# A graph network's gathers and picks: ten picked tiles, fifteen gathered ones with two pauses, and fourteen tiles in split sums

## The reference

```
h = max(layernorm(x), 0)
for i in 0, 1, 2:
    W   = (edge_attr @ ew[i] + eb[i]).reshape(E, 16, 16)
    msg = einsum('ei,eio->eo', h[src], W)
    agg = segment_sum(msg, dst, 12500)
    h   = agg + h @ rw[i] + rb[i]
    i < 2: h = relu(batchnorm(h) * gamma[i] + beta[i])    else: h = relu(h)
out = x + h @ pred_w + pred_b
```

## Time and profile before

| | |
|---|---|
| time, median of 3 runs (lowest to highest) | 7962.36 us (7962.15 to 7968.61) |
| the profiled execution: its own time, its span | 7981.32 us, 7979.3 us |
| granted clock of TensorE, mean of the span | 0.97 |
| TensorE busy | 7599.8 us (95%), 44926 matmuls |
| VectorE busy | 6861.3 us (86%) |
| GpSimd busy | 5874.3 us (74%) |
| ScalarE busy | 5047.8 us (63%) |
| bytes moved by DMA | 219.23 MB, 27 GB/s |

### The profile page before, as it was taken

One profiled execution on the slowest core, in us unless ns is written; L12 is line 12 of the kernel. 1 busy time (PEld: TensorE's weight loads), 2 busy tenths in 40 slices (PEclk: granted clock), 3 DMA queues, 4 the chain that ended last, 5 costly groups with the idle time before them and its releaser, 6 DMA issues.

```text
span 7979.3 us, 122061 instructions
## 1 busy us (share of the span) xinstructions
PE 7599.8 (95%) x44926; PEld 7163.3 (90%) x44926; DVE 6861.3 (86%) x7407; ACT 5047.8 (63%) x8079; POOL 5874.3 (74%) x6010
## 2 busy tenths in 40 slices
PE   6999999999999899999999999989999999999998
PEld 4999999899999699998999999969999999899997
DVE  6999998888888799988888888879998888888885
ACT  5666666666666566666666666656666666666664
POOL 5777777777777577777777777757777777777774
PEclk8999999999999799999999999979999999999998
DMA  4111111111111111111111111111111111111110
GB/s 42 28 28 29 28 29 27 28 28 26 28 28 26 23 30 28 28 28 28 26 28 28 27 27 28 26 24 27 30 28 28 28 28 26 28 28 26 28 26 20
DMA packets 497075, 219.23 MB, mean 27 GB/s; under 512 B 303728, under 2 KB 447728, under 8 KB 496478
## 3 DMA queue, kind: packets, MB, share of 16 engines
q1 hardware_dynamic: 255300, 159.40, 7.9%
q0 software_dynamic: 192000, 49.54, 7.6%
q10 hardware_dynamic: 49178, 2.46, 0.7%
HBM read 207.43 MB, written 3.49 MB: 26 GB/s over the span
## 4 chain that ended last, share of the span: by engine, by line
POOL 61%; issue 19%; PE 18%; DVE 1%; ACT 1%; ACTq 0%; POOLq 0%; DMA 0%; DVEq 0%
POOL xg L439 61%; PE bank L1035 10%; PE bank L991 4%; PE bank L978 1%; PE bank L988 1%; PE bank L1093 1%; PE bank L1105 1%; ACTq L804 0%; PE bank L1007 0%; PE bank L1008 0%; ACT agg L819 0%; POOLq L304 0%; ACTq L805 0%; DVE xp L586 0%; PE bank L1001 0%
## 5 line engine op out<-in xcount | busy, mean ns | idle before, releaser
L439 POOL DMA_INDIRECT xg<-node_table,idx x6000 | 5873.4, 979 | 2025.2 <-issue 1875.4
L1035 PE MATMUL bank<-nodes,low_hot 128*128 128x400 f32 x27000 | 5162.1, 349 | 78.2 <-DVE spread L631 59.2
L1035 PEld LDWEIGHTS bank<-nodes,low_hot 128*128 128x128 f32 x27000 | 4933.5, 190 | 226.9 <-DVE spread L631 129.1
L879 ACT ACTIVATE distance<-key,low_id 128x640 bf16<-128x640 int16 (+1 forms) x3000 | 2076.1, 763 | 108.9 <-ACT low_hot L883 72.9
L883 ACT ACTIVATE low_hot<-distance,one 128x640 fp32r<-128x640 bf16 (+1 forms) x3000 | 2072.1, 763 | 0.0
L631 DVE TENSOR_TENSOR spread<-mask,bank 128x400 f32<-128x400 uint8 x3375 | 1720.7, 566 | 209.8 <-PE bank L1035 209.5
L991 PE MATMUL bank<-xp,hot 128*112 128x144 f32 x13500 | 1719.1, 286 | 0.0
L586 DVE TENSOR_TENSOR xp<-xg,bank 128x3200 f32<-128x3200 f32 x375 | 1306.9, 3485 | 469.8 <-DMA xg<-node_table,idx 467.9
L991 PEld LDWEIGHTS bank<-xp,hot 128*112 128x112 f32 x13500 | 1682.0, 177 | 0.0
L843 ACT ACTIVATE xparts<-cut_room 128x1008 fp32r<-128x1008 f32 x375 | 393.6, 1050 | 1848.1 <-DVE cut_room L655 1848.1
L636 DVE TENSOR_REDUCE xg<-spread 128x80 f32<-128x2000 f32 x750 | 1521.0, 2028 | 25.6
(11 more groups left out here) (104 smaller groups left out, 1573.6 us busy)
## 6 DMA issues: line engine op xcount, KB each, us to landing
key<-edge_keys SPq DMA_DIRECT2D x375, 288.0 KB
xg<-node_table,idx POOLq DMA_INDIRECT x6000
ea<-in_edge_attr SPq DMA_DIRECT2D x375, 64.0 KB
ea<-in_edge_attr SPq DMA_DIRECT2D x375, 36.0 KB
idx<-in_src SPq DMA_DIRECT2D x375, 8.0 KB
node_table<-rows SPq DMA_DIRECT2D x3, 781.2 KB
xp<-node_table SPq DMA_DIRECT2D x9, 192.0 KB
xp<-in_x SPq DMA_DIRECT2D x2, 781.2 KB
```

What stands on the lines that cost most here:

```text
L439: pool.indirect_dma_start(out=xg[u][:, j, :], out_offset=None, in_=table[:, :], in_offset=bass.IndirectOffsetOnAxis(ap=idx[u][:, j:j + 1], ...
L879: nc.scalar.activation(distance[f][:, 0:tiles.stop - tiles.start, :], key[u % KEYS][:, tiles, :], ACT.Abs, bias=low_id[:, f:f + 1]).then_i ...
L1035: last = nc.tensor.matmul(p_sel[t % BANKS], low_hot[:, f, t, :], nodes[i][:, f, :, :].rearrange("p d f -> p (d f)"), start=(f, i) == (0, 1 ...
```

## The change

- One tile more is picked (`PICKED` 10, halves of five and five) and one fewer gathered (15).
- In each slot GpSimd stops ahead of gathers 5 and 12 (`RESTS`) until all gathers issued so far in the slot have landed. From the sixth slot of a layer on (`LEAD` = 5) it then multiplies three tiles with their features, 128x384 each time (`multiply_early`), after waiting for the sums of the slot two earlier; the first six tiles of the slot are made in this way. In the first five slots VectorE multiplies them. SyncE waits for these products too before it loads the next edges into their buffer.
- `CUT` is 14: tiles 6 to 19 are split. Their products have one buffer (`xs`), and are made and cut before the last five tiles are multiplied.
- The rest (lower part) is taken in four rounds of 504 columns. For each round ScalarE copies the upper part to PSUM (`p_cut`), and VectorE subtracts it from the products; a round waits for the one before. The rounds lie between the first four picks of the next slot.
- The transposes come after pick 4 and use bank 0, the messages after pick 7; buffers share room in other ways.

```diff
-PICKED = 9
+PICKED = 10
-CUT = 7
+CUT = 14
+ROUNDS = 4
-PARTS = (slice(0, 5), slice(5, 9))
+PARTS = (slice(0, 5), slice(5, 10))
+RESTS = (5, 12)
+EARLY = 6
+LEAD = SLOTS
...
+        xbig = sb("xbig", [P, CUTS + PAIR * WHOLES])
...
+        p_cut = bank[1][:, 0:ROUND]
...
+            def multiply_early(layer, b, u, i):
+                k = layer * G + b * SLOTS + u
+                here = slice(i * EACH, (i + 1) * EACH)
+                pool.wait_ge(s_seg, k + CREDIT - 1)
+                nc.gpsimd.tensor_tensor(
+                    xw[k % PAIR][:, here, D:D + FD].rearrange("p j (f d) -> p j f d", d=D),
+                    xg[u][:, here, :].unsqueeze(2).to_broadcast([P, EACH, F, D]),
+                    ea[u][:, here, :].unsqueeze(3).to_broadcast([P, EACH, F, D]), ALU.mult).then_inc(s_early, 1)
...
                         for j in range(FETCHED):
+                            if j in RESTS:
+                                pool.wait_ge(s_gath[u], (layer * BODIES + b) * (16 * FETCHED) + 16 * j)
+                                if b * SLOTS + u >= LEAD:
+                                    multiply_early(layer, b, u, RESTS.index(j))
                             pool.indirect_dma_start(
...
-            def multiply(layer, b, u):
+            def multiply_split(layer, b, u):
...
+                dve.wait_ge(s_xg, k * 2 + 1)
+                if k:
+                    dve.wait_ge(s_lower, ROUNDS * k)
+                products(xs, xg[u][:, SPLIT, :], p_ea[k % PAIR][:, SPLIT, :]).then_inc(s_first_prod, 1)
+
+            def multiply_whole(layer, b, u):
...
+                if b * SLOTS + u < LEAD:
+                    products(xw[k % PAIR][:, 0:EARLY, :], xg[u][:, 0:EARLY, :], p_ea[k % PAIR][:, 0:EARLY, :])
+                products(xw[k % PAIR][:, EARLY:, :], xg[u][:, LATE, :], p_ea[k % PAIR][:, LATE, :]).then_inc(s_prod, 1)
+
+            def cut_upper(k):
+                dve.wait_ge(s_xc, 2 * k + 1)
+                dve.wait_ge(s_first_prod, k + 1)
+                if k:
+                    dve.wait_ge(s_upper, k)
+                nc.vector.tensor_scalar(xcut.bitcast(I32), xbig[:, 0:CUTS].bitcast(I32), -(1 << 12), None,
                                         ALU.bitwise_and).then_inc(s_cut, 1)
+            def take_lower(k, r):
+                here = slice(r * ROUND, (r + 1) * ROUND)
+                lower = xparts[:, 1, :, :].rearrange("p a b -> p (a b)")
+                dve.wait_ge(s_round, ROUNDS * k + r + 1)
                 dve.wait_ge(s_seg, k + CREDIT)
+                nc.vector.tensor_tensor(lower[:, here], xbig[:, here], p_cut, ALU.subtract).then_inc(s_lower, 1)
...
             def copy_upper(k):
                 act.wait_ge(s_cut, k + 1)
-                nc.scalar.activation(xparts[:, :, 0, :], xcut, ACT.Copy).then_inc(s_upper, 1)
+                nc.scalar.activation(xparts[:, 0, :, :].rearrange("p a b -> p (a b)"), xcut, ACT.Copy)
+                for r in range(ROUNDS):
+                    if k + r:
+                        act.wait_ge(s_lower, ROUNDS * k + r)
+                    last = nc.scalar.activation(p_cut, xcut[:, r * ROUND:(r + 1) * ROUND], ACT.Copy)
+                    last.then_inc(s_round, 1)
+                act.wait_ge(s_round, ROUNDS * k + ROUNDS)
+                act.sem_inc(s_upper, 1)
...
+                split = range(SPLIT.start, SPLIT.stop)
+                whole = (*range(EARLY), *range(LATE.start, TILES))
+                for j in (*split[:-1], *whole, split[-1]):
```

More of the change, by code:

```diff
@@ L29 @@
 TURNS = 3
+RESTS = (5, 12)
+EARLY = 6
+LEAD = SLOTS
 WIN = 112
 NODE_P = 125
-ROOM = 3
+ROOM = 4
 SUB = 4
@@ L86, in gnn_kernel @@
         ea = [sb(f"ea{u}", [P, TILES, F]) for u in range(SLOTS)]
-        xp = [sb(f"xp{i}", [P, TILES, D + FD]) for i in range(PAIR)]
+        WIDTH = D + FD
+        CUTS, WHOLES = CUT * WIDTH, (TILES - CUT) * WIDTH
+        ROUND = CUTS // ROUNDS
+        SPLIT = slice(EARLY, EARLY + CUT)
+        LATE = slice(EARLY + CUT, TILES)
+        EACH = EARLY // len(RESTS)
+        assert EARLY == EACH * len(RESTS) and all(EACH * (i + 1) <= r for i, r in enumerate(RESTS))
+        assert FETCHED <= SPLIT.stop <= FETCHED + PARTS[0].stop
+        assert CUTS % ROUNDS == 0 and ROUND <= 512
+        xbig = sb("xbig", [P, CUTS + PAIR * WHOLES])
+        xs = xbig[:, 0:CUTS].rearrange("p (a b) -> p a b", b=WIDTH)
+        xw = [xbig[:, CUTS + i * WHOLES:CUTS + (i + 1) * WHOLES].rearrange("p (a b) -> p a b", b=WIDTH)
+              for i in range(PAIR)]
+        x_far = xbig[:, 0:CUTS + WHOLES].rearrange("p (a b) -> p a b", b=WIDTH)
         hot = [sb(f"hot{i}", [P, TILES, WIN], F32R) for i in range(PAIR)]
-        cut_room = sb("cut_room", [P, ROOM, SUB * NODE_P])
-        xcut = cut_room[:].rearrange("p a b -> p (a b)")[:, 0:CUT * (D + FD)].rearrange("p (a b) -> p a b", b=D + FD)
-        xparts = sb("xparts", [P, CUT, 2, D + FD], F32R)
+        cut_room = sb("cut_room", [P, CUTS])
+        xcut = cut_room[:]
+        assert ROOM * SUB * NODE_P <= CUTS
+        xparts = sb("xparts", [P, 2, CUT, WIDTH], F32R)
         xg = [sb(f"xg{u}", [P, TILES, D]) for u in range(SLOTS)]
-        key = [sb(f"key{i}", [P, PICKED, P], I16) for i in range(KEYS)]
+        key_all = sb("key_all", [P, KEYS, PICKED, P], I16)
+        key = [key_all[:, i, :, :] for i in range(KEYS)]
         low_hot = sb("low_hot", [P, FOLD, PICKED, P], F32R)
@@ L107, in gnn_kernel @@
         nodes = [sb(f"nodes{i}", [P, FOLD, D, FINE], F32R) for i in range(2)]
-        nodes_raw, nodes_cut = (t[:].rearrange("p a b -> p (a b)")[:, 0:FOLD * SELW]
-                                .rearrange("p (k f d) -> p k f d", k=FOLD, d=D) for t in xp)
+        NODES = FOLD * SELW
+        nodes_raw, nodes_cut = (xbig[:, i * NODES:(i + 1) * NODES].rearrange("p (k f d) -> p k f d", k=FOLD, d=D)
+                                for i in range(2))
         dst_rel = sb("dst_rel", [P, G, TILES], I16)
@@ L296, in quad_of, with early_to @@
             return layer * QUADS + g // QUAD
+        def early_to(layer, g):
+            return len(RESTS) * (layer * (G - LEAD) + max(0, g - LEAD + 1))
         def ends_quad(g):
@@ L358, in load_edges @@
                 sp.wait_ge(s_prod, layer * G + b * SLOTS + (u + 1))
+                early = early_to(layer, (b - 1) * SLOTS + u) if b else early_to(layer - 1, G - SLOTS + u) if layer else 0
+                if early:
+                    sp.wait_ge(s_early, early)
                 g = bass.ds(b * SLOTS + u, 1)
@@ L620, in set_masks, with take_picks @@
                     ALU.is_equal).then_inc(s_mask, 1)
-            def take_picks(layer, b, u, half):
+            def take_picks(layer, b, u, half, lower_of=None):
                 k = layer * G + b * SLOTS + u
@@ L634, in take_picks @@
                         p_sel[t % BANKS].rearrange("p (d f) -> p d f", d=D), ALU.mult).then_inc(s_taken, 1)
+                    if lower_of is not None and t < ROUNDS:
+                        take_lower(lower_of, t)
                 dve.wait_ge(s_taken, k * PICKED + (t1 + PICKED))
@@ L980, in _, with sum_tiles @@
             root_products(0)
-            def sum_tiles(products, onehots):
-                for j in (*range(CUT - 1), *range(CUT, TILES), CUT - 1):
-                    ends = dict(start=j == 0, stop=j == CUT - 1)
-                    if j < CUT:
+            def sum_tiles(wholes, onehots):
+                split = range(SPLIT.start, SPLIT.stop)
+                whole = (*range(EARLY), *range(LATE.start, TILES))
+                for j in (*split[:-1], *whole, split[-1]):
+                    ends = dict(start=j == split[0], stop=j == split[-1])
+                    if j in split:
                         last = nc.tensor.matmul(p_parts, onehots[:, j, :],
-                                                xparts[:, j, :, :].rearrange("p a b -> p (a b)"), **ends)
+                                                xparts[:, :, j - EARLY, :], **ends)
                     else:
-                        nc.tensor.matmul(p_z, onehots[:, j, :].bitcast(F32), products[:, j, :], **ends)
+                        nc.tensor.matmul(p_z, onehots[:, j, :].bitcast(F32), wholes[:, whole.index(j), :], **ends)
                 return last
```

105 lines of the change are left out of this document (58 added, 47 removed).

## The result

The changed kernel takes 9381.46 us (median of 4 runs, 9378.73 to 9385.79) against 7962.25 us for the kernel before beside it: 1.178 times the time, with an interval of 1.176 to 1.181. The forecast was 9400 us. GpSimd's slot, on which it rested, is a limit of this height; a second one of the same height stands beside it, which the forecast had held to be hidden, as the experiments show.

What follows compares the result with a forecast made beforehand. GpSimd's stream of gathers was taken to bound the kernel; its longer slot and layer-start stops add +498, +469 and +469 us, together +1436 on the profiled 7981.3: 9417, by the median 9395, said as 9400; range 8900 to 9900.

Steps and rivals of the forecast that it cites:

- GpSimd's slot: GpSimd's time per slot in mid-layer: fifteen gathers 18.75 us, two pauses 4.96, delayed gathers 0.4; 24.1 us, from 22.8 to 25.5.
- my three streams: GpSimd's 128x384 product: two operands read and one written, each at the iota's pace, no hold by VectorE; 1.1 us.
- Holds: Gathers delayed beside VectorE's work on SBUF: L663 goes, the cut doubles to 1.2 us; 0.4 of 0.55 us a slot stays.
- The stop at the start of a layer: GpSimd waits at gather 5 of slot 5 for TensorE's sums of slot 3: some 40 us, once a layer.
- The sum: Added time over the layers: +498 us in the first, +469 in the second and third, tail 0; together +1436 us.
- The ring: Dependency loop pick 9, ScalarE's masks and copies, VectorE's cut and rounds, pick 5, pick 9: 22.9 us, 23.2 on the mean.
- Rival (A): The loop through TensorE, ScalarE and VectorE sets the pace, the product being cheap (under 0.65 us): 9110 us; 20%.
- Rival (B): GpSimd's product costs 1.8 us or more, held by the cut or change of work: 9900 us; 14% shared with mild clock fall.
- Rival (C): Idle TensorE falls to its lower clock: 15,500 us if all work doubled (1%); mild form shares 14% with a dearer product.
- (D): The gather's 1.25 us is a transfer backlog that pauses drain, so gathers follow at 0.95 us: 7850 us at 20.2; 2%.
- (E): GpSimd's pauses find the landings past, so the change does not do what it says; 1%, shared with effects that cancel.
- Its signs of being wrong: GpSimd's products waiting for TensorE's sums in mid-layer, the chain through ScalarE's copies, or the gather pitch leaving 1.25 us.

Runs made afterwards that it cites:

- the run with pick 5 ahead: Changed kernel, pauses and products kept, VectorE taking pick 5 before its one-hot of the next slot: 9334.12 and 9371.97 us, both in disturbed sets.

## Why the prediction was right, point by point

- *GpSimd's slot, 24.1 us*: measured 23.9. The gather's pitch stayed 1.25 us. A landing wait was taken at 1.38 us with its gap where a product follows, and at 1.08 without one; 1.41 measured. The product was taken at 1.1 us and took 0.85. That term was too large by 0.25 us, and the gap behind it (0.30 taken, 0.14 found) by 0.16, 0.8 us a slot together. The product's page-based estimate, 0.85 to 1.05 us (the Trainium skill, GPSIMD Engine Reference, section 3.1 on elementwise cycle accounting), was nearer than my three streams; the trace has its low end.
- *Holds, 0.4 us*: here the error went the other way. The gathers' mean rose to 0.993, against 0.947 for one that nothing holds: 0.046 x 15 = 0.7 us a slot, and the waits for landings were longer than one row had shown (1.5 us before a product, where 2.33 - 0.95 = 1.38). The cut holds gathers as the forecast said, 1.36 us beside it above, but by more: the 487 gathers beside it took 1.42 us in the mean, 0.6 us a slot. Errors of both signs left 0.2 us of the slot, so that 9400 was met this closely is in part luck.
- *The stop at the start of a layer*: "some 40 us". 34.6 us in the second layer, 35.3 in the third and 58.3 in the first; the sums of slot 3 were done 3338.0 - 3181.6 = 156.4 us into it, forecast 153.2.
- *The sum*: +1436 us on the profiled execution forecast, 9376.9 - 7979.3 = +1398 in the spans.
- *"Against GpSimd's 24.1 it stays hidden, by 0.9 us"*: this step failed. The ring was worked out at 22.9 and 23.2 us and measured at 23.2 us for a turn, but at 23.85 on the mean, because TensorE's clock falls when it waits for pick 5's bank. The prediction had put "a few lower stretches" into TensorE's idle time; they fall on pick 9 itself, where TensorE is on the ring. The two limits are equal within 0.1 us, and the time was the same without the pauses (9378 us): the pauses and products to which the forecast put the rise add nothing to it while the ring stands. That GpSimd's slot by itself gives the same time is what the run with pick 5 ahead shows.
- *Rival (A), the ring sets the pace*: as true as the forecast. It gave 9110 us from turns of 23.2 us; with 23.85 its sum gives some 9350. The prediction's sentence that "even a free product could not hold the old time" is what the run without pauses shows.
- *Rival (B)*: no. The product takes 0.84 to 0.85 us in the mean of 750 and of 720, and the next gather starts 0.14 us after it, so no change of work on GpSimd shows.
- *Rival (C)*: in its mild form yes, at pick 9. *(D)*: no, by the waits alone, after which the pitch is 1.25 us. *(E)*: no.
- *Its signs of being wrong*: the pitch held, and TensorE's wait before pick 9 ends with L679, as said. GpSimd does not wait for TensorE's sums in mid-layer. But the chain does run through ScalarE's copies, and that sign told of the second limit rightly.
- *What was not seen*: that ten picks alone cost 17% in the old order too, by the timeline through another ring, over the sums and the next five picks. The prediction had named the bank ("tile 8 needed tile 4"), but looked for its cost only in the new order, where the ring goes through ScalarE's rounds.

## What to carry to other kernels

When work is shifted between engines, count what a buffer's turn comes to: one more item than the banks allow can tie the end of one engine's batch to the start of the other's, and cost more than its own work (3.6 us a slot for the tenth pick alone, whose matmuls take 1.5, with a gather saved). When a chain through GpSimd, VectorE, ScalarE and TensorE has no owner, take away one suspect at a time and then both; a limit that is hidden by 0.1 us looks like no limit in every single test. And a long wait of TensorE (3.1 us here, not 1.5) is paid twice where the first matmuls after it are on the path.

## What the runs showed of the hardware that was not expected

On the chips of two of the five sets of runs the kernel before took 11338 us (11323 to 11397, 7 runs) and 11601 us (11586 to 11623, 7 runs), where it took 7948 to 7978 in the others (7981 in the profiled execution). It was so in every execution. Each disturbed set had a chip of its own, so what the chip does and what the hour does are not taken apart. In those two sets the kernels without pauses took 12176, 12138 and 11687 us, and those with a landing wait twice a slot 9435, 9334 and 9372 us. So there the kernels with the change's pauses are 17 to 19% faster than the kernel before, and not 18% slower, as the changed kernel is elsewhere. The changed kernel itself was not timed there, and no kernel with pauses was timed on both kinds of chip: that these kept their time is judged by what was expected of them.

Two kernels were profiled on both kinds, the changed one without pauses and that one with pick 5 ahead. TensorE's whole-tile sums in the first, first on the disturbed chip, then on the other:

```profile
L1071 PE MATMUL bank<-xbig,hot 128*112 128x144 f32 x8250 | 1740.9, 344 | 1272.7 <-issue 1261.3 <-DVE spread L677 0.9
```
```profile
L1071 PE MATMUL bank<-xbig,hot 128*112 128x144 f32 x8250 | 1076.8, 287 | 0.0
```

On the disturbed chip TensorE stands for 1261 us in gaps ahead of matmuls that wait for nothing the profile shows; in the other kernel they are 1912 us, and none on the undisturbed chip. Its timeline there, at the end of a run of fifteen gathers:

```profile
1508.21 0.65 PE L1071 MATMUL bank<-xbig,hot 128*112 128x144 f32 x4
1509.43 0.94 POOL L484 DMA_INDIRECT xg<-node_table,idx  x1 [0.30 <-issue]
1510.10 0.40 PE L1071 MATMUL bank<-xbig,hot 128*112 128x144 f32 x2 [1.23 <-issue]
1510.67 0.94 POOL L484 DMA_INDIRECT xg<-node_table,idx  x1 [0.30 <-issue]
1511.50 0.28 PE L1071 MATMUL bank<-xbig,hot 128*112 128x144 f32 x1 [1.00 <-issue]
```

One or two matmuls go through for each gather, until 3 us after the last one; VectorE and ScalarE stand until 1514.3 ahead of instructions that wait for pick 9, whose matmuls TensorE had finished by 1506.6. What holds TensorE is open. The three profiled kernels with unbroken runs of gathers have 1261 to 1912 us of such gaps ahead of their sums; the two with landing waits have 7 us or less there, and 176 to 425 us ahead of their picks, where the changed kernel on its own chip has next to none. So two landing waits a slot go with far smaller gaps, not with none. No profile of the kernel before was taken there.
